# Scheduling the row maxima of the first batch inside its attention, and the loads of the last pass inside the last taps

## The reference

```python
attn = softmax(einsum('bhnd,bhmd->bhnm', q, k) * SCALE)
x = x + proj(einsum('bhnm,bhmd->bhnd', attn, v))
y = deform_conv(gn(x), offset, mask, proj_w, proj_b)      # y of one batch
yn = (y - y.mean(axis=(0, 2, 3))) * rsqrt(y.var(axis=(0, 2, 3)) + 1e-05)
out = x + gelu(yn * gamma + beta)
```

## Time and profile before

| | |
|---|---|
| median of 3 executions | 3497.58 us |
| profiled execution, its own time | 3496.99 us |
| its span, first to last instruction | 3495.2 us |
| mean granted TensorE clock | 0.978 |
| start section, to the first scores of batch 0 | 157.87 us |
| attention of batch 0, steps 0 to 43 | 157.87 to 225.10 us |
| last matmul of the last taps ends | 3418.05 us |
| DMA traffic in all | 97.25 MB |

### The profile page before, as it was taken

One profiled execution on the slowest core, in us unless ns is written; L12 is line 12 of the kernel. 1 busy time (PEld: TensorE's weight loads), 2 busy tenths in 40 slices (PEclk: granted clock), 3 DMA queues, 4 the chain that ended last, 5 costly groups with the idle time before them and its releaser, 6 DMA issues. The chain is left out here.

```text
span 3495.2 us, 84765 instructions
## 1 busy us (share of the span) xinstructions
PE 3234.6 (93%) x33434; PEld 1895.0 (54%) x33434; DVE 2340.7 (67%) x3770; ACT 1670.6 (48%) x2700; POOL 1323.7 (38%) x1183
## 2 busy tenths in 40 slices
PE   5899999999999999999999999999999999998991
PEld 2265555555555555555555555555555555554660
DVE  5976677666776677866768667776677667765443
ACT  4274344644455443654437444464445544364443
POOL 0172334523354332723337233452335433263430
PEclk9799999999999999999999999999999999998995
DMA  4000000000001000000000000000000000001007
GB/s 140 19 3 37 19 1 21 2 37 19 2 21 38 1 19 2 21 38 2 20 21 3 37 19 1 21 2 37 19 2 22 38 1 1 2 21 73 1 2 325
DMA packets 12146, 97.25 MB, mean 28 GB/s; under 512 B 2813, under 2 KB 2941, under 8 KB 5008
## 3 DMA queue, kind: packets, MB, share of 16 engines
q1 hardware_dynamic: 9504, 67.40, 5.1%
q0 software_dynamic: 1152, 12.58, 0.9%
q10 hardware_dynamic: 1008, 11.01, 0.8%
HBM read 56.26 MB, written 34.60 MB: 26 GB/s over the span
## 5 line engine op out<-in xcount | busy, mean ns | idle before, releaser
L1618 PE MATMUL R<-P,WALL 128*128 128x512 f16 x3888 | 980.4, 378 | 0.3 <-issue 0.3
L636 POOL TENSOR_TENSOR PL<-P 128x1024 f16<-128x1024 f32 x256 | 617.3, 2417 | 483.7 <-ACT P L810 481.0
L1051 DVE TENSOR_REDUCE MXP<-G 128x1 f32<-128x512 f32 x926 | 631.7, 688 | 158.7 <-PE G L1375 152.0
L1597 PE MATMUL R<-MHL,XB 128*128 128x240 f16 (+14 forms) x7776 | 718.7, 234 | 2.4 <-DVE P L1291 2.4
L672 POOL TENSOR_TENSOR MHL<-M,MHL 128x280 f16<-128x280 f32 (+2 forms) x576 | 366.6, 638 | 787.5 <-ACT MHL L905 786.4
L1597 PEld LDWEIGHTS R<-MHL,XB 128*128 128x128 f16 x7776 | 580.3, 98 | 98.6 <-DVE P L1291 2.7
L810 ACT ACTIVATE P<-R 128x1024 f32<-128x1024 f32 x512 | 520.6, 1022 | 200.3 <-PE R L1420 200.1
L1618 PEld LDWEIGHTS R<-P,WALL 128*128 128x128 f16 x3888 | 377.5, 97 | 393.1 <-issue 0.5
L1123 DVE TENSOR_TENSOR PL<-P 128x1024 f16<-128x1024 f32 x256 | 487.2, 1908 | 97.2 <-ACT P L810 96.9
L1420 PE MATMUL R<-QK 48*128 48x512 f16 (+1 forms) x3072 | 422.7, 381 | 18.9 <-ACT P L810 15.6
L1268 DVE TENSOR_TENSOR M<-G,PL 128x240 f32<-128x240 f32 (+17 forms) x864 | 249.7, 319 | 271.3 <-ACT PL L895 148.3
(11 more groups left out here) (146 smaller groups left out, 3530.5 us busy)
## 6 DMA issues: line engine op xcount, KB each, us to landing
XA<-x SPq DMA_DIRECT2D x8, 1536.0 KB, 6.3
X<-x SPq DMA_DIRECT2D x8, 1536.0 KB, 6.9
x_scratch<-X SPq DMA_DIRECT2D x7, 1536.0 KB, 5.1
y_scratch<-XP ACTq DMA_DIRECT2D x7, 1536.0 KB, 5.1
WALL<-y_scratch SPq DMA_DIRECT2D x6, 1536.0 KB, 14.7
out<-WALL POOLq DMA_DIRECT2D x6, 1536.0 KB, 10.8
QK<-x_scratch SPq DMA_DIRECT2D x4, 1536.0 KB, 17.3
P<-wd SPq DMA_DIRECT2D x9, 576.0 KB, 4.9
```

The source lines that it names most:

```text
L636: pool.tensor_tensor(PL[:, s % P_BUFS, :], P32[:, s % P_BUFS, :], high_view(s), ALU.subtract).then_inc(p_low_pool, 1)
L1051: dve.reduce_max(MXP[:, name[1] % 2, n // 2, n % 2:n % 2 + 1], chunk(sec, name)[:, :], AX.X).then_inc(dve_read, 1)
L1597: last = pe.matmul(out, XT[:, x_part, g * BOX_Y + r, t * 128:(t + 1) * 128], MHL[:, m_part, o + at:o + at + (hi - lo) * (x1 - x0)], start= ...
L1618: last = pe.matmul(R6[:, CT + ct, :], WALL[:, w:w + 128], PHL[:, u % 2, part // 2, t, :], start=(u % TAPS == 0 and n < CT), stop=(u % TAPS ...
```

## The change

In the start section only the 32 maxima of pair 0 are left. The 96 of pairs 1 to 3 go into the attention of batch 0, 9 in 4 steps (2, 2, 2, 3), in steps 0 to 42, in the two banks that chunks of attention use; their `maxT` stand in steps 15, 29 and 43. In batch 0 the low halves of steps below 44 are split one in three to DVE (15 steps) and two in three to POOL (29 steps). The row DMAs of pairs 1 to 3 and `heads_alone` of pair 3 move with them.

In the last pass each `k` has a place of its own for `x1` and for `y`, put together from buffers that are dead by then, in up to three pieces; only `y` of `k = 7` reuses `YS`, and a third of its `x1` reuses `X1`. The seven `x1` are issued (but for that third) where four were issued before. `y` of `k = 1` and `2` are issued after the convolution of unit 15 of the last batch (`taps_used`), those of 3 to 6 after the last convolution (`y_full`, no longer the statistics), that of 7 after `out` of `k = 0` is done. `added` counts single tiles, and the last `out` goes in three pieces.

```diff
+def first_fills():
+
+    maxima, fills, due = MAXIMA[4 * QT:], [[] for _ in range(STEPS)], []
+    for s in range(STEPS):
+        fills[s], due = due, []
+        count = 9 * (s + 1) // 4 - 9 * s // 4
+        due = [("maxT", n[1]) for n in maxima[:count] if n[2] == 4 * QT - 1]
+        fills[s], maxima = fills[s] + maxima[:count], maxima[count:]
+    return fills
...
+def step_chunks(s, start, first=False):
+
+    out = list(FIRST_FILL[s]) if first else []
+    out += [TRANSPOSE_AT[s]] if s in TRANSPOSE_AT else []
...
-    maxima = list(MAXIMA)
+    maxima = MAXIMA[:4 * QT]
     for n in range(4, len(QK)):
         out += [QK[n]] + maxima[:3]
         maxima = maxima[3:]
-    for name in maxima:
-        out.append(name)
-    for i in range(PAIRS):
-        last = out.index(MAXIMA[4 * QT * (i + 1) - 1])
-        out.insert(min(last + 5, len(out)), ("maxT", i))
-    return with_readers(out)
-
-
-def batch_chunks(start):
-
-    out = sum((step_chunks(s, start) for s in range(STEPS)), [])
+    return with_readers(out + [("maxT", 0)])
...
-DVE_STEPS = [s for s in range(STEPS) if s % 2 == 0]
-POOL_STEPS = [s for s in range(STEPS) if s not in DVE_STEPS]
+POOL_STEPS = [s for s in range(STEPS) if s % 2]
+FIRST_POOL = [s for s in range(STEPS) if (s % 3 if s < 44 else s % 2)]
...
+        X_AT = [[X1F], [places(QKF, 0)], [places(QKF, 2 * CT * PIX)], [XR.rearrange("p t n -> p (t n)")],
+                [places(VS[:, :, :, :].rearrange("p q h d -> p (q h d)"), 0)],
+                [places(QKF, 4 * CT * PIX, 2), places(WALL, WVO, 1)], [places(QZF, 0, 2), places(WPF, 0, 1)],
+                [places(WQKF[:, :], 0, 2), X1F[:, 0:PIX]]]
+        Y_AT_END = [[YSF], [places(WALL, 0)], [places(WALL, 4 * CT * PIX)], [places(WALL, 2 * CT * PIX)],
+                    [places(XB[:, :, :, :].rearrange("p a t n -> p (a t n)"), 0)],
+                    [P32[:, 0:CT, :].rearrange("p t n -> p (t n)")], [places(PLF, 0, 2), places(MHLF, 0, 1)], [YSF]]
...
-            rows_and_next(start_section(), 1, True)
+            rows_and_next(start_section(), 1, True, range(1))
+            rows_and_next(before_taps(0), 1, False, range(1, PAIRS))
...
-            for k in range(1, min(XS, BATCH)):
-                sp.dma_start(XF(k), x1_d[FINAL[k], :, :]).then_inc(xf_in[k % XS], 16)
-            sp.wait_ge(y_stats, BATCH)
-            if BATCH > 1:
-                sp.wait_ge(y_out, BATCH * 16)
+            def final_x(k, pieces):
+
+                for a, cols in pieces:
+                    sp.dma_start(a, x1_d[FINAL[k], :, cols]).then_inc(xf_in[k], 16)
+
+            def final_y(k):
+
+                for a, cols in pieces_of(Y_AT_END[k]):
+                    sp.dma_start(a, y_d[FINAL[k], :, cols]).then_inc(yf_in[k], 16)
+
             for k in range(1, BATCH):
-                if k >= 4:
-                    sp.wait_ge(out_done[k % 4], 16 * (k // 4))
-                sp.dma_start(YF(k), y_d[FINAL[k], :, :]).then_inc(yf_in[k % 4], 16)
-                if k >= XS:
-                    sp.wait_ge(added, k - XS + 1)
-                    sp.dma_start(XF(k), x1_d[FINAL[k], :, :]).then_inc(xf_in[k % XS], 16)
+                final_x(k, pieces_of(X_AT[k])[:1 if k == BATCH - 1 else None])
+            sp.wait_ge(y_out, 16 * 3)
+            sp.wait_ge(taps_used, 1)
+            for k in (1, 2):
+                final_y(k)
+            sp.wait_ge(y_out, BATCH * 16)
+            sp.wait_ge(y_full, 2 * BATCH)
+            for k in range(3, BATCH - 1):
+                final_y(k)
+            sp.wait_ge(added, CT)
+            final_x(BATCH - 1, pieces_of(X_AT[BATCH - 1])[1:])
+            sp.wait_ge(out_done[0], 16)
+            final_y(BATCH - 1)
...
+            for k in range(BATCH - 1):
+                pool.wait_ge(added, (k + 1) * CT)
+                for a, cols in pieces_of(Y_AT_END[k]):
+                    pool.dma_start(out[FINAL[k], :, cols], a).then_inc(out_done[k], 16)
+            k = BATCH - 1
+            for t in range(CT):
+                pool.wait_ge(added, k * CT + t + 1)
+                pool.dma_start(out[FINAL[k], :, t * PIX:(t + 1) * PIX], final_tile(Y_AT_END[k], t)).then_inc(out_done[k], 16)
             for k in range(BATCH):
-                pool.wait_ge(added, k + 1)
-                pool.dma_start(out[FINAL[k], :, :], YF(k)).then_inc(out_done[k % 4], 16)
...
+                    for name in step_chunks(s, not final, is_first(b)):
                         read_chunk(name, sec, b)
+                        if name[0] == "maxT" and name[1] + 2 < PAIRS:
+                            heads_alone(sec, name[1] + 2, b)
...
+                    dve.tensor_tensor(y, y, final_tile(X_AT[k], t), ALU.add).then_inc(added, 1)
...
+                        if final and u == UNITS - 3 and end == CONVS:
+                            last.then_inc(taps_used, 1)
```

More of the change, by code:

```diff
@@ L185, in start_chunks, with batch_chunks @@
         maxima = maxima[3:]
-    for name in maxima:
-        out.append(name)
-    for i in range(PAIRS):
-        last = out.index(MAXIMA[4 * QT * (i + 1) - 1])
-        out.insert(min(last + 5, len(out)), ("maxT", i))
-    return with_readers(out)
-def batch_chunks(start):
-    out = sum((step_chunks(s, start) for s in range(STEPS)), [])
+    return with_readers(out + [("maxT", 0)])
+def batch_chunks(start, first=False):
+    out = sum((step_chunks(s, start, first) for s in range(STEPS)), [])
     out += (DRAIN if start else []) + [("oT", CT - 1, 1)]
@@ L223 @@
 START = start_chunks()
-BEFORE_TAPS, LAST_BEFORE = batch_chunks(True), batch_chunks(False)
+FIRST_BEFORE, BEFORE_TAPS, LAST_BEFORE = batch_chunks(True, True), batch_chunks(True), batch_chunks(False)
 if (len(BEFORE_TAPS) + len(tap_chunks(NEAR_OFF, True))) % 2:
     BEFORE_TAPS = [(("pass", ""), "", 1)] + BEFORE_TAPS
+    FIRST_BEFORE = [(("pass", ""), "", 1)] + FIRST_BEFORE
+FIRST_MORE = sum((with_readers(fills) for fills in FIRST_FILL), [])
 PER_BATCH = BEFORE_TAPS + tap_chunks(NEAR_OFF, True)
@@ L276, with pool_steps, pool_lows, dve_lows @@
             raise ValueError("both reaches must count alike")
-DVE_STEPS = [s for s in range(STEPS) if s % 2 == 0]
-POOL_STEPS = [s for s in range(STEPS) if s not in DVE_STEPS]
+POOL_STEPS = [s for s in range(STEPS) if s % 2]
+FIRST_POOL = [s for s in range(STEPS) if (s % 3 if s < 44 else s % 2)]
+def pool_steps(b):
+    return FIRST_POOL if is_first(b) else POOL_STEPS
+def pool_lows(b, s):
+    earlier = 0 if is_first(b) else b * len(POOL_STEPS) + len(FIRST_POOL) - len(POOL_STEPS)
+    return earlier + pool_steps(b).index(s) + 1
+def dve_lows(b, s):
+    earlier = 0 if is_first(b) else b * (STEPS - len(POOL_STEPS)) + len(POOL_STEPS) - len(FIRST_POOL)
+    return earlier + [k for k in range(STEPS) if k not in pool_steps(b)].index(s) + 1
 START_LINKS, BATCH_LINKS = 3, 15
@@ L474, in build, with places, pieces_of, final_tile @@
         QKF = QK4[:, :, :, :].rearrange("p a i n -> p (a i n)")
[L475 to L478, removed]
+        X1F, YSF = [a.rearrange("p t n -> p (t n)") for a in (X1[:, :, :], YS[:, :, :])]
         FINAL = [BATCH - 1] + list(range(BATCH - 1))
[L484 to L492, removed]
+        def places(a, first, tiles=CT):
+            return a[:, first:first + 2 * tiles * PIX].bitcast(fp32)
+        WPF = WP[:, :, :, :].rearrange("p a t n -> p (a t n)")
+        QZF, MHLF = QZ[:, :, :, :].rearrange("p a d n -> p (a d n)"), MHL[:, :, :].rearrange("p a n -> p (a n)")
+        X_AT = [[X1F], [places(QKF, 0)], [places(QKF, 2 * CT * PIX)], [XR.rearrange("p t n -> p (t n)")],
[5 more added lines that the diff above has]
+                    [P32[:, 0:CT, :].rearrange("p t n -> p (t n)")], [places(PLF, 0, 2), places(MHLF, 0, 1)], [YSF]]
+        def pieces_of(areas):
+            out, t = [], 0
+            for a in areas:
+                n = a.shape[1] // PIX
+                out.append((a, slice(t * PIX, (t + n) * PIX)))
+                t += n
+            return out
+        def final_tile(areas, t):
+            for a, cols in pieces_of(areas):
+                if cols.start <= t * PIX < cols.stop:
+                    return a[:, t * PIX - cols.start:(t + 1) * PIX - cols.start]
         SELF = SEL[:, :, :].rearrange("p a n -> p (a n)")
@@ L569, in x1_done, with rows_and_next @@
                 sp.wait_ge(dve_read, before_taps(b, final).at(PROJ[-1], "D"))
-            def rows_and_next(sec, b, more):
-                for i in range(PAIRS):
+            def rows_and_next(sec, b, more, pairs=range(PAIRS)):
+                for i in pairs:
                     sp.wait_ge(act_read, sec.at(("maxT", i), "A"))
@@ L631, in batch @@
             def batch(b, final):
-                for s in POOL_STEPS:
+                for s in pool_steps(b):
                     pool.wait_ge(p_exp, b * STEPS + s + 1)
@@ L1105, in batch @@
                     if s < STEPS:
-                        for name in step_chunks(s, not final):
+                        for name in step_chunks(s, not final, is_first(b)):
```

(2 more changed lines are left out.)

41 lines of the change are left out of this document (21 added, 20 removed).

## The result

The changed kernel takes **3468.1 us** (median of 4 executions, 3466.6 to 3470.6), the kernel before 3497.7 us in the same comparison: a ratio of 0.9916 [0.9899, 0.9933], 29.6 us faster. The forecast was 3460 us, 37.6 us under the median before. The profiled execution has 3467.78 us, its span 3466.0 us, its mean granted clock is 0.985.

A forecast was written before the change was run, and what follows sets the result against it. DVE was taken to bound the start, PE attention of batch 0 (DVE after the change), transfers the last pass. -56.3 + 42 - 23.9 = -38.2 us gave a median of 3459.4, rounded up to 3460 us; range 3444 to 3480.

The forecast's parts named there:

- The start: Start section: 96 maxima leave a section bound by DVE, first scores at 101.6 us instead of 157.87, -56.3 us.
- Attention of batch 0: Steps 0 to 43 of batch 0: 109.5 us instead of 67.2, +42 us (+34 to +60).
- 7 of the 22 low halves go to POOL, at 1.90 us each: Attention of batch 0: takes 13.3 us off DVE's work, which sums to 101.5 us.
- The first rival: Attention of batch 0: PE stays the bound, growth of 21 to 25 us, 3440 us in all; chance 8%.
- DVE becomes the bound: Attention of batch 0, steps 0 to 43: DVE has 101.5 us of work against PE's 88.
- I take the nearer end, 5 us for the 11 steps with three: Attention of batch 0: bank waits in steps with three tiles cost 5 us beyond DVE's 101.5 us of work.
- The far end: Attention of batch 0: upper bound for bank waits, DVE idle at its share of before, 101.5 / 0.80 = 127 us.
- The row wait of pair 1: Attention of batch 0, step 16: scores wait for the rows some 3 us past PE's turn.
- The clock: Attention of batch 0: granted clock taken as 0.97, that of this attention before the change.
- the slower rival: Attention of batch 0: the clock falls, 179 us instead of 109.5 at half, 3530 us; decides from 0.60; chance 4%.
- The last pass: Last matmul to the end: earlier loads leave 20.97 MB, 50.4 us at 416 GB/s, -23.9 us.
- the rival of the bank waits: Attention of batch 0: DVE idles at its share of before, 127 us, +60, so 3478 us; chance 13%.

The follow-up runs named there:

- late_third: Changed kernel with chunks of a step after the second issued on PE behind the value products, same work on every engine: 3460.6 us.
- late_quarter: `late_third` with low halves of batch 0's steps below 44 on DVE only every fourth step, 11 instead of 15: 3453.2 us.
- end_only: Changed kernel with the start section and low-half split of before, so only the last pass is changed: 3474.8 us, ratio 0.9935.
- start_only: Changed kernel with the last pass of before, so only the start section and attention of batch 0 are changed: 3490.7 us, ratio 0.9977.
- old_split: Changed kernel with batch 0's low halves split between DVE and POOL in turn, 22 on DVE instead of 15 in 44 steps: 3473.1 us.
- early36_late: Changed kernel with 36 maxima in the start section, the others two a step, and chunks after the second behind the value products: 3456.4 us.
- late_third_busy: `late_third` with 8 more zero-matrix products on PE ahead of the first scores: 3459.8 us, one execution.
- y12_late: Changed kernel with `y` of `k` = 1 and 2 issued only after the last convolution: 3475.8 us, one execution.

## Why the prediction came out as it did

**The start (forecast -56.3, measured -57.4): right.** The issues of the two rows end at 99.21 us and the scores start at 100.43 us, 1.2 us after, where 2 us was taken between 0 and 3.7.

**Attention of batch 0 (forecast 109.5 us, measured 113.9): the size is near, but by luck. Two errors nearly cancelled: DVE has 10.7 us less work than was counted (90.8 for 101.5) and idles 23.1 us where 8 were (5 for the steps with three, 3 for the row wait).**
- The step "7 of the 22 low halves go to POOL, at 1.90 us each" together with "busy now 53.65 us" priced the remaining 15 at 1.90 us too. They take 1.23 (group above). 15 times 0.67 us is 10 us: 101.5 becomes 91.5, measured 90.8. The first rival had named this ("low halves shrink by themselves, 1.2 us without POOL beside them") and the sum hadn't used it.
- "DVE becomes the bound" is the step that failed. It predicted DVE busy over 90%; it is 80%, and a step with two maxima takes PE's 1.90 us when nothing else asks for DVE or a bank.
- "I take the nearer end, 5 us for the 11 steps with three" was the term of the sum that was mis-sized: less the row wait, DVE idles some 20 us and not 5. There are ten such steps and not 11 (steps 3, 7, ... 39), and they take 21.8 us more than PE's work, the row wait among them. The choice of the near end rested on DVE's queue being full, and it wasn't. The far end took DVE's idle share of before, and that share came out the same: 90.8 / 0.80 = 113.9 us. No run shows a reason why it should; before, DVE idled because PE was the bound, and with the same chunks in another order (`late_third`) or fewer low halves on DVE (`late_quarter`) its busy share is 85% and 86%. `late_third` shows that part of this wait comes from the order on PE.
- The row wait of pair 1 came where it was forecast and a little shorter, about 2 us for 3: PE waits twice for `QK<-MR`, 1.6 us at the first scores and 1.9 at step 16. But 5.70 us from exponential to exponential is what step 15 costs, with its bank wait.
- The clock: forecast 0.97, measured 0.91. It stands at half from 101.0 to 114.6 us, then again from 121.5 to 124.9 and from 145.4 to 148.8, and not once after that. Before the second fall PE was idle from 119.8 to 121.4 us (x0 in 120:121 above), waiting for a bank; before the third, for the rows of step 16, from 143.2 to 145.2. Not every such wait is followed by a fall: 1.57 us of idle PE from 131.0 us were not, nor were 1.80 us from 137.0 us in `late_quarter`. The Trainium skill ("TensorE: Matmul & The Clock Gate", section "A second HAM failure mode: psum-queue depth-cycling") describes this kind of swing between the levels; the trace agrees that it happens, with 20 of 114 us at half clock. It stays far from the 0.60 at which the slower rival decides.

**What lies between (forecast 0, measured +4.2 us): missed.** The first exponentials of the batches, after against before, are at -11.0 in step 44 of batch 0 and then -10.6, -10.3, -9.9, -9.5, -9.2, -8.9 and -7.3 us in batches 1 to 7. The early loads of the last pass are not the cause: from step 44 to the last matmul `end_only`, which has them, loses 0.3 us and `start_only`, which doesn't, 2.7. The runs narrow it down further, by the same reading:
- 0.3 to 0.4 us per batch in `start_only` and `late_third`, 0.16 on average in `late_quarter`, 0.05 or less in `end_only`, and 0.0 in `old_split`. So it goes with the new split of batch 0's low halves, though the programs of the later batches issue the same work. The mechanism stays open.
- 1.2 us in attention of batch 6: 97.7 us from first to last exponential, against 96.5 before; batches 1 to 5 have 97.6 to 97.7 in both. So before, batch 6 was the odd one. The other runs have 97.6 to 97.8 there, but for `early36_late` (99.2) and `late_third_busy` (96.6). Why stays open.

**The last pass (forecast -23.9, measured -22.4): right, by its own steps; the 1.5 us missed are mostly the tail, 3.0 us from the end of the full flow to that of the span, where 1.3 was taken.** 50 us of full DMA engines at 412 GB/s are 20.6 of the 20.97 MB that were counted. The last gelu waited 4.0 us for its `y` (3446.36) and the queues stayed full behind it, so that cost nothing. The 358 GB/s that the Trainium skill gives as a core's share ("DMA: Bandwidth & Descriptors", section "Where 436 GB/s comes from") would have made this 58.6 us; the trace speaks against it again. `y12_late` confirms the price of a load: 3.7 us each for two, where 3.8 was taken.

The sum missed by 9 us of the profiled execution: +4.4 in attention, +4.2 between, +1.5 at the end, less 1.1 in the start. The time lies inside the range, about halfway between the forecast and the rival of the bank waits (3478 us).

## What to carry to other kernels

When work of one engine is handed to another through two buffers, price the step in which a third is needed by what stands ahead of the read on the other engine, and put that producer last in its step's order: moving the third chunk behind the 24 value products was worth 8 us over 44 steps, an estimated 2 of them by the clock. When both engines are busy well under all the time and each idles for the other, look for such a handover, and don't price it by the idle share of another bound: that share was 20% here, and 12% to 19% in variants of the same stretch. Here the last pass, bound by transfers, was costed in bytes to within 1.5 us; where its last dependent load was issued behind 4.2 MB more, it took 3.4 us over its bytes.

## What the runs showed of the hardware

- A two-input subtraction of 128x1024 on DVE takes 1.21 to 1.23 us when POOL makes none at its start, and longer when POOL is at one of its own. This pair is from the trace of the kernel before:

```profile
169.68 2.47 POOL L636 TENSOR_TENSOR PL<-P 128x1024 f16<-128x1024 f32 x1 [0.37 <-ACT P L810]
...
171.10 2.13 DVE L1123 TENSOR_TENSOR PL<-P 128x1024 f16<-128x1024 f32 x1
```

  POOL's ends at 172.15 us and DVE's at 173.23, 1.08 us later. Nine such meetings between 163 and 197 us, all that overlap by more than 0.1 us, end 1.07 to 1.09 us apart, whether DVE's took 1.54 or 2.31 us: DVE's hardly got on while POOL's ran. The other way round, POOL's takes 1.89 us alone (104.87 us in the changed kernel), and 2.65 where it starts 0.32 us into one on DVE (190.41 us before), ending 1.75 us after that one. The Trainium skill ("SBUF — State Buffer", section "SBUF: two separate sides") says that two-input DVE operations and POOL hold a shared pair of ports against each other. The trace agrees. So it is the meeting in time that costs, not the share of each engine: `old_split` gives DVE the old share in slower steps and has a mean of 1.26 us, against 1.90 in the earlier trace rows.
- In each of the runs with the new start TensorE's clock goes to the lower level once or more in the 44 steps, each time behind or in a wait of PE: 1.6 us of waiting for rows were followed by 13.6 us at half clock in the changed kernel. In `start_only`, whose attention is the same program, it fell three times more and not twice (0.50 in the windows 144 to 148 and 196 to 200 us); there the 44 steps took 3.7 us longer. By windows of 1 us, 30.7 us at half clock stand against 20.5 in the changed kernel. So the same waits aren't followed by the same falls in two executions, and variants are compared fairly only with the time at half clock beside their times.
- A batch whose own program is the same ran some 0.4 us slower where batch 0 was split otherwise (above), by a mechanism that no run shows.
